# Latent attention beside a gated feed-forward on one core: rope steps spread over the units, swaps between the transposes, two score spans handled as one

## What is computed

```
xn  = layernorm(x)                                   # x: 2048 x 256
q   = (xn @ wq) as 16 heads of 128 (nope) + 64 (rope)
ckv, k_pe = split(xn @ wkv_a)                        # 64 + 64
ckv = ckv * rsqrt(mean(ckv^2) + eps) * kv_norm_scale
k_nope, v = split(ckv @ wkv_b)                       # per head 128 + 128
q_pe, k_pe = rope(q_pe), rope(k_pe)
attn = softmax(causal(q k^T * 192^-0.5))
s   = (attn @ v as 2048 x 2048) @ wo
g   = silu((silu(xn@gate_w.T * gate_s) * (xn@up_w.T * up_s)) @ down_w.T * down_s)
out = x + s * g
```

## Time and profile before

| | us |
|---|---|
| three runs, median (lowest to highest) | 1090.41 (1087.71 to 1095.07) |
| the profiled execution | 1087.01 |
| its span, from first to last instruction | 1085.2 |

### The profile page before, as it was taken

The page is one execution under the profiler, slowest core; times in us unless marked ns, Lnnn a source line. Parts: engine busy times, 40 slices in busy tenths (PEclk is TensorE's granted clock), DMA queues, the critical chain, the costliest instruction groups (busy, mean ns, idle before and its releaser), DMA issues.

```text
span 1085.2 us, 26363 instructions
## 1 busy us (share of the span) xinstructions
PE 965.5 (89%) x10560; PEld 829.1 (76%) x10560; DVE 758.7 (70%) x1095; ACT 757.9 (70%) x1093; POOL 793.0 (73%) x576
## 2 busy tenths in 40 slices
PE   5659798999889989999999899999899987989998
PEld 5637687788778777877787787877787776877887
DVE  5748578787878687768786787778677875852134
ACT  1428687788778787878787878878688875863222
POOL 3667979697969796979697969887788889623331
PEclk7869999999999999999999999999899998989999
DMA  5019999999999999999999999999999999992001
GB/s 170 10 49 168 161 188 170 195 172 175 172 194 165 177 176 193 178 172 176 193 174 170 186 183 181 168 170 182 189 148 187 178 171 211 201 166 79 1 20 59
DMA packets 591979, 170.24 MB, mean 157 GB/s; under 512 B 574064, under 2 KB 585968, under 8 KB 591856
## 3 DMA queue, kind: packets, MB, share of 16 engines
q1 hardware_dynamic: 587376, 167.89, 86.6%
q10 hardware_dynamic: 4480, 0.66, 0.4%
HBM read 15.41 MB, written 2.10 MB: 16 GB/s over the span
## 4 chain that ended last, share of the span: by engine, by line
POOL 34%; PE 30%; SPq 9%; DMA 9%; issue 6%; DVE 6%; ACT 5%; ACTq 1%; POOLq 0%
POOL hl L1114 16%; PE s_ps L529 10%; PE s_ps L627 9%; DMA pT<-hl 5%; SPq L472 5%; PE slot_ps L529 4%; POOL pe L1114 4%; POOL q_swap L1114 3%; SPq L464 3%; POOL QB_lo L1114 2%; POOL QA_lo L1114 2%; ACT hl L733 2%; POOL QB_hi L1114 2%; POOL QA_hi L1114 2%; DMA q_swap<-q_pe 2%
## 5 line engine op out<-in xcount | busy, mean ns | idle before, releaser
L1114 POOL TENSOR_TENSOR hl<-prob,hl 128x1024 f16<-128x1024 f32 (+4 forms) x256 | 417.5, 1631 | 134.0 <-ACT hl L733 120.1
L806 ACT ACTIVATE prob<-s_ps,neg_max 128x1024 f32<-128x1024 f32 (+7 forms) x384 | 317.5, 861 | 71.3 <-DVE neg_max L948 44.2
L733 ACT ACTIVATE hl<-prob 128x1024 f16<-128x1024 f32 (+7 forms) x384 | 296.3, 804 | 79.2 <-DMA pT<-hl 76.5
L945 DVE TENSOR_REDUCE part_max<-s_ps 128x1 f32<-128x1024 f32 (+7 forms) x256 | 244.6, 986 | 142.2 <-PE s_ps L627 124.2
L643 PE MATMUL o_ps<-v,pT 128*128 128x65 f16 x2176 | 228.7, 193 | 18.8 <-DMA pT<-hl 14.2
L644 PE MATMUL o_ps<-v,pT 128*128 128x64 f16 x2176 | 229.1, 196 | 0.0
L645 PE MATMUL o_ps<-v,pT 128*128 128x65 f16 x2176 | 227.8, 192 | 0.0
L643 PEld LDWEIGHTS o_ps<-v,pT 128*128 128x128 f16 x2176 | 204.5, 97 | 20.9 <-DMA pT<-hl 15.3
L954 DVE TENSOR_TENSOR hl<-prob,hl 128x1024 f16<-128x1024 f32 (+3 forms) x128 | 190.1, 1485 | 37.9 <-ACT hl L733 36.4
L645 PEld LDWEIGHTS o_ps<-v,pT 128*128 128x128 f16 x2176 | 203.9, 99 | 0.0
L644 PEld LDWEIGHTS o_ps<-v,pT 128*128 128x128 f16 x2176 | 203.2, 97 | 0.0
(11 more groups left out here) (183 smaller groups left out, 1950.3 us busy)
## 6 DMA issues: line engine op xcount, KB each, us to landing
q_swap<-q_pe SPq DMA_DIRECT2D x128, 64.0 KB, 2.2
pT<-hl SPq DMA_TRANSPOSE x256, 5.1
wq_sb<-in_L_attn_wq_dram SPq DMA_DIRECT2D x8, 384.0 KB, 4.2
acc<-in_L_attn_x_dram SPq DMA_DIRECT2D x4, 512.0 KB, 6.3
wo_sb<-in_L_attn_wo_dram SPq DMA_DIRECT2D x8, 256.0 KB, 3.4
x_in<-in_L_attn_x_dram SPq DMA_DIRECT2D x1, 2048.0 KB, 9.6
out_dram<-y SPq DMA_DIRECT2D x8, 256.0 KB, 2.1
wkvs<-in_L_attn_wkv_b_dram SPq DMA_DIRECT2D x8, 128.0 KB, 4.0
```

Source lines behind the costliest of these rows:

```text
L733: return nc.scalar.activation(dst, src, ACT.Copy)
L806: nc.scalar.activation(prob_of(u, m), score_bank(u, m), ACT.Exp, bias=neg_max[:, r:r + 1]).then_inc(exp_done, 1)
L945: nc.vector.tensor_reduce(part_max[:, u % 2, m:m + 1], src, AX.X, ALU.max).then_inc(part_done, 1)
L1114: return lambda: nc.gpsimd.tensor_tensor(dst, a, b, op)
```

## The change

- POOL's steps are spread anew: at most two full steps in a unit but for units 6 and 14, one of them between `low` and `rest`. `wpe_hi` and `wpe_lo` come in units 3 and 4 instead of 6. The copies to `pe_b` and the last splits come one unit later.
- `q_pe` gets two buffers and `pe_b` one instead of two.
- In a unit with a swap, SP issues the swap after `turn_first` and before `turn_rest`.
- Spans 1 and 2 lie side by side in `hl12`: 1152 high columns, then 1152 low ones. ACT rounds both in one operation. DVE makes the low half of columns 0 to 831, POOL of columns 832 to 1151, in every unit.
- At the first unit of a pair TensorE makes the scores of span 1 behind the weighing of span 0.
- In the last pair the ffn steps and loads come one unit later, and `outP1b` moves into the tail.

```
-FFN_COUNT = {7: 1, 8: 1, 9: 2, 10: 2, 12: 1, 14: 2, 15: 2}
+FFN_COUNT = {8: 1, 9: 2, 10: 2, 12: 1, 13: 1, 14: 2, 15: 2}
-POOL_NEXT = {1: ["wkvs"], 6: ["wpe_hi", "wpe_lo"], 9: rope(3)[:1], 10: rope(3)[1:], 11: rope(0)[:1] + side("A", 3), 12: rope(0)[1:] + ["B3hi"],
-             13: ["B3lo"] + side("A", 0), 14: side("B", 0)}
+POOL_NEXT = {1: ["wkvs"], 3: ["wpe_hi"], 4: ["wpe_lo"], 9: ["rope3.0"], 10: ["rope3.1", "rope3.2"], 11: side("A", 3), 12: ["rope0.0", "B3hi"],
+             13: ["rope0.1", "rope0.2"], 14: side("A", 0) + ["B3lo"], 15: side("B", 0)}
...
-POOL = Steps(POOL_SETUP + [name for u in range(NU) for name in [("low", u), ("rest", u)] + steps_at(u)])
+POOL = Steps(POOL_SETUP + [name for u in range(NU) for name in [("low", u)] + steps_at(u)[:1] + [("rest", u)] + steps_at(u)[1:]])
...
-        q_pe = ab("q_pe", [P, BANK])
+        q_pe = ab("q_pe", [P, 2, BANK])
...
+                turn_first(u)
                 for name in jobs_at(u - 1):
                     if name[0].startswith("qB"):
                         swap(int(name[0][2:]), name[1])
-                turn_first(u)
                 turn_rest(u)
...
+                first = (u + 1) % PU == 0
                 if u + 1 < NU:
                     scores(u + 1, 0)
-                    scores(u + 1, 1)
+                    if not first:
+                        scores(u + 1, 1)
                 if u >= LAG:
                     weigh(u - LAG, 0)
                 if u + 1 < NU:
+                    if first:
+                        scores(u + 1, 1)
                     scores(u + 1, 2)
...
-                    if n >= 1:
-                        before = GROUP_ORDER[(n - 1) % NG], (n - 1) // NG
-                        act.wait_ge(swapped, 64 * n)
+                    if n >= 2:
+                        before = GROUP_ORDER[(n - 2) % NG], (n - 2) // NG
+                        act.wait_ge(swapped, 64 * (n - 1))
...
+            def rest_high(u):
+
+                act.wait_ge(exp_done, scores_through(u, 2))
+                if u >= 2:
+                    act.wait_ge(turned12[u % 2], turned_count(u - 2))
+                copy(hl12[:, u % 2, 0:W12], prob12[:, u % 2, :]).then_inc(prob_hi, 1)
...
+            def prob_low(u):
+                dve.wait_ge(prob_hi, 2 * u + 2)
+                nc.vector.tensor_tensor(hl12[:, u % 2, W12:W12 + DVE_LOW], prob12[:, u % 2, 0:DVE_LOW], hl12[:, u % 2, 0:DVE_LOW], ALU.subtract).then_inc(lo_dve, 1)
...
+            def rest_low(u):
+                run(("rest", u), tt(hl12[:, u % 2, W12 + DVE_LOW:2 * W12], prob12[:, u % 2, DVE_LOW:W12], hl12[:, u % 2, DVE_LOW:W12], ALU.subtract),
+                    (prob_hi, 2 * u + 2))
```

More of the change, by code:

```diff
@@ L132 @@
 JOBS_FIRST = {0: ["qA2"]}
[L133 removed]
+FFN_COUNT = {8: 1, 9: 2, 10: 2, 12: 1, 13: 1, 14: 2, 15: 2}
 EARLY = {PU * PAIRS - 1: (0, 2), PU * PAIRS: (2, 4)}
[L136 removed]
+OUT_LAST = {j: (name, PAIRS - 1) for j, name in ((0, "outP1b"), (1, "outT2"), (2, "outP2a"), (3, "outP2b"), (5, "outT3"), (7, "outP3a"), (8, "outP3b"))}
 def jobs_at(u):
@@ L457, in swap @@
                     a, b = slice(i * half, (i + 1) * half), slice((i ^ 1) * half, (i ^ 1) * half + half)
-                    sp.dma_start(q_swap[a, :], q_pe[b, :]).then_inc(swapped, 16)
+                    sp.dma_start(q_swap[a, :], q_pe[b, n % 2, :]).then_inc(swapped, 16)
             def turn_first(u):
@@ L495, in _ @@
                     load_wo(pair + 1)
-                if pair == PAIRS - 1 and k == 4:
+                if pair == PAIRS - 1 and k == 5:
                     load_ffn()
@@ L642, in weigh @@
                     kb = first_key(m) // P + b
-                    nc.tensor.matmul(whole, pT[:, b, :], v[:, kb, 0:LORA + 1], start=(m != 1 and b == 0), stop=False)
-                    nc.tensor.matmul(part, pT[:, b, :], v[:, kb, LORA + 1:VW], start=False, stop=False)
-                    last = nc.tensor.matmul(whole, pT[:, n + b, :], v[:, kb, 0:LORA + 1], start=False, stop=(m > 0 and b == n - 1))
+                    nc.tensor.matmul(whole, pT_hi[:, b, :], v[:, kb, 0:LORA + 1], start=(m != 1 and b == 0), stop=False)
+                    nc.tensor.matmul(part, pT_hi[:, b, :], v[:, kb, LORA + 1:VW], start=False, stop=False)
+                    last = nc.tensor.matmul(whole, pT_lo[:, b, :], v[:, kb, 0:LORA + 1], start=False, stop=(m > 0 and b == n - 1))
                 last.then_inc(pv_done, 1)
@@ L1136, in rope_step @@
                     done = ((queries_split, n - 1),) if 2 <= n < 4 else ()
-                    run((name, pair), tt(turned, q_pe[:], cosT[:, query_cols(g)], ALU.mult), (hi_done, after("hi", (f"qB{g}", pair))),
+                    run((name, pair), tt(turned, q_pe[:, n % 2, :], cosT[:, query_cols(g)], ALU.mult), (hi_done, after("hi", (f"qB{g}", pair))),
                         (tables_loaded[g], 32), *done)
@@ L1244, in _ @@
             for u in range(NU):
-                prob_low(u, 0)
-                prob_low(u, smaller(u))
-                for name in steps_at(u):
+                first_low(u)
+                for name in steps_at(u)[:1]:
+                    step(name)
+                rest_low(u)
+                for name in steps_at(u)[1:]:
                     step(name)
```

58 lines of the change are left out of this document (25 added, 33 removed).

## The result

The changed kernel takes 1062.57 us (median of 4 runs, 1060.36 to 1067.65); beside them the kernel before took 1090.62. The ratio is 0.9746, with an interval of 0.9695 to 0.9797: 28 us faster, where 34 were forecast (1056 us), and within the range of 1028 to 1093. The profiled execution has a span of 1058.6 us, against 1085.2 before.

What follows compares the result with a forecast made beforehand. DMA, through SyncE's queue, was taken as the nearest floor; closing 4.9 us of SP's breaks a pair gives 35 us, less 0.8 us for the tail, so 1056 us from 1090.4, range 1028 to 1093.

Steps and rivals of the forecast that it cites:

- The ceiling by SP's breaks: SyncE's queue: the gain is what its breaks lose, 7.3 us a pair less 2.4 staying, 4.9 us a pair.
- TensorE's waits alone: Rival: TensorE alone is the bound, so all 64.8 us of its waits are won, 1026 us; chance 0.12.
- nothing moves: Rival: SP's breaks fill but its issues lengthen by as much, 7.3 us; time 1085 us, chance 0.18.
- DMA as the floor: DMA engines: 19.9 MB a pair at 190 GB/s takes 104.6 us, the nearest floor, allowing 7.1 us a pair.
- `wc_lo`, 12.8 us: Weight split at steps 3 and 4 instead of 6: removes TensorE's wait of 12.8 us in 7 places.
- `q_pe`, 15.9 us: Two q_pe halves: ACT's 26.4 us of swap waits go, with six TensorE waits for exponentials, together 15.9 us.
- POOL's steps, 36.1 us as one of three terms: Units with three POOL steps exceed 6.98 us; spreading them should remove most of TensorE's remaining 36.1 us of waits.
- Halves at 0: Low halves parted at 832: DVE's mean stays 1.485 us, gain 0; bounds 0 to 38 us lost.
- The slower rival: POOL stands before the swap in units 2 and 10, 30 us of waits; 1107 us, chance 0.15.
- POOL waiting over 1 us in units 2 and 10: Sign that the forecast is wrong: POOL waits for q_swap<-q_pe over 1 us a unit there.
- ACT's waits for `pT` under 30 us: Sign that the forecast is right: ACT's waits for pT<-hl fall from 62 to under 30 us.
- The ffn loads: Last pair: loads come one unit later with the same 10 DMAs; the 5.98 us wait stays, within 2 us.

Runs made afterwards that it cites:

- swap_first: The changed kernel with SP issuing the swap ahead of the unit's first transpose again; ratio 0.9705 to the kernel before.
- one_swap: The changed kernel with one swap transfer of 128 rows instead of four of 32, leaving out the halves' exchange; 1049.99 us, ratio 0.9631.
- early_wpe: The kernel before with only the weight split (wpe_hi, wpe_lo) moved from unit 6 to units 3 and 4; 1094.01 us, ratio 1.0021.
- tables_one_q_pe: The kernel before with only the changed step tables, last pair's included, and its single q_pe buffer; 1067.47 us, ratio 0.9767.
- rope_behind: The changed kernel with both rope steps behind POOL's rest of the low half in units 2 and 10; ratio 0.9711 to the kernel before.

## Why the prediction was right, point by point

**The ceiling by SP's breaks** was the step that carried the number, and it held in kind: 4.9 us a pair were to close, and 8.5 - 3.4 = 5.1 closed. That the two agree so well is partly luck. I had counted 7.3 us in one pair where the mean is 8.5, and left 2.4 where 3.4 stayed. The remainder was also misplaced: I expected breaks of 0.3 us in some 8 units, and 19.0 of some 24 us stand in units 7 and 8. By TensorE's waits alone the forecast would have been 1026 us.

**The term of the sum that was mis-sized** is what a closed break is worth. I set it 1 to 1 (35 us). The pair fell by 3.25 us, 26 us in all. SP's issues grew meanwhile: a swap group from 2.56 to 2.91 us in the mean (x4 a pair, 1.4 us), the first transpose from 2.13 to 2.30 (x16, 2.7), the second fell from 3.35 to 3.20 (x16, -2.4), together 1.7 us, near the 5.1 - 3.25 = 1.85 missing. That is a part of the rival "nothing moves", which had 7.3. A part of the growth goes with the swap's new place: in swap_first the group is at 2.59 us and the first transpose at 2.19.

**DMA as the floor** was right in its place and wrong in its name. I took 190 GB/s of the engines, 104.6 us a pair. What limits is SP's time: by the means of the changed kernel 16 x 2.30 + 16 x 3.20 + 4 x 2.91 = 99.6 us, and some 0.1 us between two issues and three weight loads of about 0.5 us beside it. one_swap took from this alone and became faster. That 104.6 came near the 108.25 - 3.4 = 104.85 us of SP's time was chance.

**`wc_lo`, 12.8 us:** the wait went as forecast, the worth was wrong alone (early_wpe: none). I had written that what comes next would have been waiting already; POOL's units 3 and 4, into which the step moved, were the crowded ones. I had counted "POOL's work is the same" and not in which unit.

**`q_pe`, 15.9 us:** the wait went; alone it is worth 5 us, with the tables none that can be measured.

**POOL's steps, 36.1 us as one of three terms:** the mechanism, three steps a unit over 6.98 us and POOL falling behind, was right, and it carries nearly all of the 28 us (tables_one_q_pe). The right measure is a unit of SP's queue, 6.44 us, not one of the pair's period.

**Halves at 0:** right, within a few us. DVE's `hl` took 1.490 us (1.485 forecast), POOL's 320 columns 1.03 us (1.1 taken); the contention that spoke against it did not raise DVE's mean. My reading of it was wrong. At 513.9 POOL's `hl` ran beside DVE's 1.22 us too, from 514.01 on, and at 521.2 DVE took 2.14 us where POOL's had begun before it, at 520.15. What differs is which of the two began first (see the last section).

**The slower rival** came about as a wait, nearly as priced (32.9 us in 13 places, 30 in 15 forecast), and hardly reached TensorE. Its point of decision, 13 us of 30, was not met: swap_first, rope_behind and both together put its cost at 0 to 5. "POOL waiting over 1 us in units 2 and 10" was thus a sign that did not tell the slower case.

**ACT's waits for `pT` under 30 us** was wrong, with 91.5, and should not have been forecast by one who held the queue for the bound: where the queue is full, whoever waits for it waits longer. A second `q_pe` buffer took a wait from ACT and raised this one, from 59.2 to 97.5 us without the tables and from 55.9 to 80.8 with them. DMA's mean was 183 GB/s, not 188, and a pair 108.25 us, not 107.

**The ffn loads:** the 5.98 us of the earlier trace rows became 3.16 us. The forecast was the same within 2 us, which was 0.8 too narrow.

**Not tried:** the scores' new order at a pair's first unit, the step between POOL's low halves, and the later `outP1b` by themselves. As tables_one_q_pe lacks the first two and stands at 0.9767, they can be worth only a few us together. The later `outP1b` is in it, so its 0.8 us stays untested.

## What to carry to other kernels

Where one in-order queue is nearly full, sum the work of the engine that feeds it unit by unit, and compare each unit with the queue's own time for one: the same total, spread so that no run of units is over, was worth 2.3% here, while removed waits of 12 to 33 us were worth 0 to 0.5% each. Count the time between the feeding engine's operations too: at 0.08 us each it made 3 of the 9 us of excess here. A wait that is removed moves to another name unless it is one of those that leave breaks in the queue. And count the issues on a DMA queue, not only its bytes: before a transfer is made in four parts, or given to a compute engine to issue, price each at its issue time.

## What the hardware showed that I had not expected

- An issue of a 64 KB transfer and one of 256 KB hold SP for the same time (medians 0.586 and 0.542 us), and when the issues of the swaps went, the transposes' did not stretch.
- Half the columns cut a transpose's mean issue on SP from 2.30 to 1.37 us, and the other one, unchanged, fell with it from 3.20 to 2.85. So the time of an issue depends on its own size and on what is issued around it.
- The same group of four small transfers held ACT for 3.3 us, and SP for 2.4 to 3.0.
- When DVE's low half and a POOL operation overlap, the one that begins second takes longer, and the first keeps its time in nearly all places. In the changed kernel POOL's 320 columns took 1.45 us or more in all 42 places where DVE's low half was already running when they began, and 0.80 in the 86 others, in 11 of which DVE began while they ran. The 0.67 us lost is near the 0.8 us that DVE's operation still had to run. It holds the other way round too: DVE's 832 columns took 1.01 to 1.03 us in the 29 places where POOL ran nothing as they began, and up to 2.76 where they began behind a `low`, while the 57 `low` of those places kept their 2.13 to 2.16 us. One place shows both, POOL first, then DVE:

```profile
554.22 2.14 POOL L1122 TENSOR_TENSOR hl<-prob,hl 128x1024 f16<-128x1024 f32 x1
556.44 1.70 POOL L1122 TENSOR_TENSOR QA_hi<-pe,ones 64x512 fp32r<-64x512 f32 x1
558.22 0.80 POOL L1122 TENSOR_TENSOR hl<-prob,hl 128x320 f16<-128x320 f32 x1
```

```profile
554.58 2.66 DVE L962 TENSOR_TENSOR hl<-prob,hl 128x832 f16<-128x832 f32 x1
```

DVE began behind POOL's `hl` and took 2.66 us; `QA_hi` began behind DVE's and took 1.70, where it takes 1.03 elsewhere. As the step now stands between the low halves, it pays this price, and the 320 columns here, at 0.80, do not (their mean is 1.03); the sum of a pair stays at 92 us.
